# The high and low parts of the embedding rows: made per use by ScalarE and VectorE, or once by GpSimd and loaded

## The reference, cut to what matters

```
x1 = relu(x @ W_ah + b_ah)
for W, a_src, a_dst, b in the three layers:
    h = (x1 @ W).reshape(N, 4, 192)                  # the feature product
    e = leaky_relu((h*a_src).sum(-1)[src] + (h*a_dst).sum(-1)[dst], 0.2)
    p = exp(e - segment_max(e, dst)[dst]); alpha = p / segment_sum(p, dst)[dst]
    out = relu(segment_sum(alpha * h[src], dst) + b)
x = x + relu(concat(outs) @ W_out + b_out) + linear_attention(layernorm(x))
```

## Time and profile before

| | us |
|---|---|
| median of three runs | 1359.35 |
| the profiled execution itself | 1361.11 |
| its span in the trace | 1359.3 |
| TensorE busy | 1292.5 (95%) |
| VectorE busy | 984.1 (72%) |
| ScalarE busy | 509.4 (37%) |
| GpSimd busy | 44.1 (3%) |

### The profile page before, as it was taken

The page is one execution under the profiler, slowest core; times in us unless marked ns, Lnnn a source line. Parts: engine busy times, 40 slices in busy tenths (PEclk is TensorE's granted clock), DMA queues, the critical chain, the costliest instruction groups (busy, mean ns, idle before and its releaser), DMA issues.

```text
span 1359.3 us, 19970 instructions
## 1 busy us (share of the span) xinstructions
PE 1292.5 (95%) x7893; PEld 1220.7 (90%) x7893; DVE 984.1 (72%) x1703; ACT 509.4 (37%) x844; POOL 44.1 (3%) x52
## 2 busy tenths in 40 slices
PE   5899889999997999999999999999999999999886
PEld 5667559999996999999999999999999999999784
DVE  5667859999997526967766676677667766778577
ACT  4334232434345214443334333433343334333373
POOL 5000000000000500000000000000000000000000
PEclk9999989999998999999999999999999999999998
DMA  9210030222215847102011102110211011105003
GB/s 248 86 71 1 1 110 20 92 92 78 88 39 164 239 125 197 38 14 66 1 73 38 41 0 74 39 41 1 74 38 41 0 73 39 43 1 149 1 0 114
DMA packets 23510, 90.13 MB, mean 66 GB/s; under 512 B 3537, under 2 KB 4878, under 8 KB 20347
## 3 DMA queue, kind: packets, MB, share of 16 engines
q1 hardware_dynamic: 22495, 86.57, 19.9%
q10 hardware_dynamic: 924, 2.30, 0.6%
HBM read 77.80 MB, written 11.06 MB: 65 GB/s over the span
## 4 chain that ended last, share of the span: by engine, by line
PE 54%; DVE 7%; ACT 1%; issue 0%; DVEq 0%
PE psum L1763 26%; PE psum L105 9%; PE psum L106 8%; PE psum L107 8%; DVE hN L1383 2%; PE psum L1777 1%; DVE prob L1367 1%; DVE prob L1361 1%; PE psum L1817 1%; DVE acc L1500 0%; DVE acc L1405 0%; DVE x1l L1390 0%; PE psum L1832 0%; DVE acc L1421 0%; ACT prob L1591 0%
## 5 line engine op out<-in xcount | busy, mean ns | idle before, releaser
L1763 PE MATMUL psum<-hN,prob 125*125 125x193 f32 x2400 | 408.8, 327 | 0.0
L1763 PEld LDWEIGHTS psum<-hN,prob 125*125 125x125 f32 x2400 | 395.4, 187 | 0.2
L1591 ACT ACTIVATE prob<-prob,acol 125x1250 f32<-125x1250 f32 x120 | 160.9, 1341 | 378.8 <-DVE prob L1361 378.8
L1367 DVE SCALAR_TENSOR_TENSOR prob<-prob,cnt 125x1250 f32<-125x1250 f32 x120 | 174.6, 1455 | 56.3 <-ACT prob L1591 56.3
L1361 DVE SCALAR_TENSOR_TENSOR prob<-vrow,ncol,urow 125x1250 f32<-125x1250 f32 x120 | 181.7, 1515 | 9.5 <-PE psum L1763 9.5
L796 DVE CUSTOM_DVE_ANT_0 junk<-mask,arow 125x1250 bf16<-125x1250 uint8 x120 | 174.7, 1456 | 3.1
L105 PE MATMUL psum<-woh,xlh 128*125 128x384 f32 x360 | 128.0, 356 | 2.6 <-DVE acc L1405 2.6
L106 PE MATMUL psum<-wol,xlh 128*125 128x384 f32 x360 | 123.3, 343 | 0.0
L107 PE MATMUL psum<-woh,xll 128*125 128x384 f32 x360 | 122.6, 341 | 0.0
L105 PE MATMUL psum<-wph,x1h 128*125 128x384 f32 x330 | 117.6, 356 | 3.4 <-PEq L1018 1.9
L107 PE MATMUL psum<-wph,x1l 128*125 128x384 f32 x330 | 111.3, 337 | 0.0
(11 more groups left out here) (255 smaller groups left out, 2128.9 us busy)
## 6 DMA issues: line engine op xcount, KB each, us to landing
arow<-scratch_a SPq DMA_DIRECT2D x12, 625.0 KB, 3.9
urow<-scratch_uv SPq DMA_DIRECT2D x12, 625.0 KB, 4.4
vrow<-scratch_uv SPq DMA_DIRECT2D x12, 625.0 KB, 5.9
wT<-in_w_turned SPq DMA_DIRECT2D x6, 1152.0 KB, 7.4
wq_raw<-in_w_qkv SPq DMA_DIRECT2D x6, 1152.0 KB, 6.7
wp_raw<-in_w_pair SPq DMA_DIRECT2D x6, 1152.0 KB, 7.5
wo_raw<-in_w_out SPq DMA_DIRECT2D x6, 1152.0 KB, 5.3
xN<-in_x SPq DMA_DIRECT2D x10, 336.0 KB
```

The lines of the kernel that those rows point to most:

```text
L1367: nc.vector.scalar_tensor_tensor(prob[n % RING][:, :], prob[n % RING][:, :], 1.0, cnt[:, n % NT, :], op0=ALU.min, op1=ALU.mult).then_inc(p ...
L1591: nc.scalar.activation(prob[n % RING][:, :], prob[n % RING][:, :], ACT.Exp, bias=acol[:, n // NT, n % NT:n % NT + 1]).then_inc(e_ready, 1)
L1763: last = nc.tensor.matmul(bank(t // 2)[0:P, 193 * (t % 2):193 * (t % 2) + 193], ring[:, t * P:(t + 1) * P], hN[i % 2][:, j, 193 * s:193 * ...
```

## The change

The parts of the ten tiles of `x1` are made once. During attention GpSimd makes for each tile a high part (a cast) and a low part (a subtraction) in one buffer, `x1_in_store`, and SyncE stores it to device memory (`dram_x1`, 6000 bytes for each of 128 partitions, 750 KB a tile). GpSimd starts a tile when the store of the one before has landed. In the convolutions ScalarE starts a load of 750 KB for each feature product but the first, into two buffers in turn (`x1_both`), one of them where `x1T` was. `x1_high` and `x1_low` are gone from ScalarE and VectorE. A load waits until the product that last read its buffer is done.

```
--- before.py
+++ after.py
@@ -116,6 +116,7 @@
     dram_a, dram_low = scratch("a", (HEADS, N)), scratch("low", (HEADS, 1))
     dram_uv = scratch("uv", (2 * HEADS, N))
     dram_y = scratch("y", (PAIRS, 128, N))
+    dram_x1 = nc.dram_tensor("scratch_x1", (NT, 128, 2 * KT * P), F32, kind="Internal").ap()
     dram_res = scratch("res", (NT, P, D))
     ctx = ExitStack()
     with ctx:
@@ -162,8 +163,11 @@
         y_next = at("y_next", STAGE_AT + 41312, [128, N])
         wp_first = at("wp_raw", ACC_AT + 4 * NT * D + 99520, [128, KT * PC])
 
-        x1h = at("x1h", MASK_AT, [128, KT, P], F32R)
-        x1l = at("x1l", MASK_AT + 3008, [128, KT, P], F32R)
+        x1_in_store = at("x1_in_store", STAGE_AT + 68960, [128, 2 * KT * P])
+        x1_store = [x1_in_store[:, KT * P * q:KT * P * (q + 1)].bitcast(F32R).rearrange("p (k n) -> p k n", k=KT) for q in range(2)]
+        x1_both = [at(f"x1_both{b}", o, [128, 2 * KT * P]) for b, o in enumerate((MASK_AT, X1_AT))]
+        (x1h, x1l), (x1h_odd, x1l_odd) = [[both[:, KT * P * q:KT * P * (q + 1)].bitcast(F32R).rearrange("p (k n) -> p k n", k=KT)
+                                           for q in range(2)] for both in x1_both]
         wph = at("wph", ACC_AT + 4 * NT * D + 71104, [128, KT, PC], F32R)
         wpl = at("wpl", ACC_AT + 4 * NT * D + 99520, [128, KT, PC], F32R)
 
@@ -696,7 +700,7 @@
 
 
     at, xnh, xnl, mask, amax, bank = (g[k] for k in "at xnh xnl mask amax bank".split())
-    ident = g["ident"]
+    ident, x1T = g["ident"], g["x1T"]
     with ExitStack() as ctx:
         def sb(name, shape, dt=F32):
             return ctx.enter_context(nc.sbuf_tensor(name, shape, dt))
@@ -704,6 +708,7 @@
         def sem(name):
             return ctx.enter_context(nc.semaphore(name))
 
+        parts_ready, parts_out = sem("parts_ready"), sem("parts_out")
         w_raw, w_high, w_low = g["wq_raw"], g["wq_high"], g["wq_low"]
         S = STAGE_AT
         kf = at("kf", S, [P, NT, 128])
@@ -752,16 +757,23 @@
                 sp.wait_ge(y_ready, NG * (i + 1))
                 sp.dma_start(g["dram_y"][i], y[:, :]).then_inc(y_out, 16)
 
+            def store_parts(t):
+                sp.wait_ge(parts_ready, 2 * t + 2)
+                sp.dma_start(g["dram_x1"][t], g["x1_in_store"][:, :]).then_inc(parts_out, 16)
+
             a_row(0)
             a_row(1)
             for i in range(PAIRS):
                 if i + 1 < PAIRS:
                     weights(i + 1)
+                    store_parts(2 * i)
                     a_row(2 * i + 2)
                 if i:
                     store(i - 1)
                 if i + 1 < PAIRS:
                     a_row(2 * i + 3)
+                    store_parts(2 * i + 1)
+            sp.wait_ge(parts_out, 16 * NT)
             for k in range(2):
                 sp.dma_start(g["wp_first_raw"][k][:, :], g["w_proj"][:, PROJ[k], :]).then_inc(g["wproj_in"][k], 16)
             sp.wait_ge(y_out, 16)
@@ -780,6 +792,14 @@
                 nc.gpsimd.memset(blocks[b, 128 + h:129 + h], 1.0).then_inc(zeroed, 1)
                 pool.wait_ge(zeroed, 2 * h + 3)
             nc.gpsimd.memset(vf[:, :, 128:130], 1.0).then_inc(ones_col, 1)
+            high, low = g["x1_store"]
+            for t in range(NT):
+                here = x1T[:, :, t * P:(t + 1) * P]
+                if t:
+                    pool.wait_ge(parts_out, 16 * t)
+                nc.gpsimd.tensor_copy(high[:, :, :], here).then_inc(parts_ready, 1)
+                pool.wait_ge(parts_ready, 2 * t + 1)
+                nc.gpsimd.tensor_tensor(low[:, :, :], here, high[:, :, :].bitcast(F32), ALU.subtract).then_inc(parts_ready, 1)
 
         @block.vector
         def _(dve):
@@ -1206,8 +1226,8 @@
         S = ACC_AT + 4 * NT * D
 
         hN = [at(f"hN{i}", S + 15456 * i, [P, NT, PC + 2]) for i in range(2)]
-        x1h_odd = at("x1h_odd", S + 15456, [128, KT, P], F32R)
-        x1l_odd = at("x1l_odd", S + 15456 + 3008, [128, KT, P], F32R)
+        x1h_odd, x1l_odd, x1_both = (g[k] for k in "x1h_odd x1l_odd x1_both".split())
+        x1_in = [sem(f"x1_in{b}") for b in range(2)]
         gN = [h[:, :, 1:PC + 1] for h in hN]
         prob = [at(f"prob{i}", S + 30912 + 5024 * i, [P, N]) for i in range(RING)]
         urow = [at(f"urow{i}", S + 51008 + 10048 * i, [128, N]) for i in range(2)]
...
@@ -1270,8 +1290,8 @@
         def down_of(t):
             return max(d for d, (t0, n) in enumerate(DOWNS) if t0 <= t)
 
-        def x1_parts(i, t):
-            return (x1h_odd, x1l_odd) if i == 0 and t % 2 else (x1h, x1l)
+        def x1_parts(t):
+            return (x1h_odd, x1l_odd) if t % 2 else (x1h, x1l)
 
 
         @block.sync
@@ -1384,12 +1404,6 @@
                                                    total[:, t // 2, t % 2:t % 2 + 1], b_pair[0:P, C * s:C * (s + 1)],
                                                    op0=ALU.mult, op1=ALU.add).then_inc(g_ready, 1)
 
-            def x1_low(i, t):
-                dve.wait_ge(xh_ready, NT * i + t)
-                high, low = x1_parts(i, t)
-                nc.vector.tensor_tensor(low[:, :, :], x1T[:, :, t * P:(t + 1) * P], high[:, :, :].bitcast(F32), ALU.subtract)\
-                    .then_inc(xl_ready, 1)
-
             def out_low(i, t):
 
                 dve.wait_ge(t_high, NT * i + t + 1)
@@ -1513,8 +1527,6 @@
                         scores(tile + AHEAD)
                     if 0 <= i and tile + AHEAD - 1 < ALL:
                         weigh(tile + AHEAD - 1)
-                    if i + 1 < PAIRS and n >= NT and (i, n) not in ((-1, NT), (0, NT)):
-                        x1_low(i + 1, n - NT)
                     if i >= 1 and 2 <= n < NT + 2:
                         accumulate(i - 1, n - 2)
                     if 0 <= i and not lean and tile + AHEAD < ALL:
@@ -1526,8 +1538,6 @@
                     if i == -1 and EARLIER + AHEAD <= n < EARLIER + 2 * AHEAD - 1:
                         weigh(n - EARLIER - AHEAD)
                     if 0 <= i and n == NT - 1:
-                        if i == 0:
-                            x1_low(1, 0)
                         denominators(i, 0)
                         normalise(i, 0, range(NT))
                     if i >= 0 and n == TILES - 1:
@@ -1591,12 +1601,10 @@
                 nc.scalar.activation(prob[n % RING][:, :], prob[n % RING][:, :], ACT.Exp,
                                      bias=acol[:, n // NT, n % NT:n % NT + 1]).then_inc(e_ready, 1)
 
-            def x1_high(i, t):
-                if i:
-                    act.wait_ge(h_full, NT * i + t)
-                elif t >= 2:
-                    act.wait_ge(h_full, t - 1)
-                nc.scalar.activation(x1_parts(i, t)[0][:, :, :], x1T[:, :, t * P:(t + 1) * P], ACT.Copy).then_inc(xh_ready, 1)
+            def x1_load(i, t):
+                if NT * i + t >= 2:
+                    act.wait_ge(h_full, NT * i + t - 1)
+                act.dma_start(x1_both[t % 2][:, :], g["dram_x1"][t]).then_inc(x1_in[t % 2], 16)
 
             def take_h(i, t):
                 act.wait_ge(h_full, NT * i + t + 1)
@@ -1670,18 +1678,18 @@
                 for n in range(TILES):
                     tile = TILES * i + n
                     if i + 1 < PAIRS and n >= NT:
-                        if (i, n) not in ((-1, NT), (0, NT)):
-                            x1_high(i + 1, n - NT)
                         if n > NT:
                             take_h(i + 1, n - NT - 1)
+                        if n + 1 < TILES:
+                            x1_load(i + 1, n - NT + 1)
+                    if 0 <= i < PAIRS - 1 and n == NT - 1:
+                        x1_load(i + 1, 0)
                     if 0 <= i < PAIRS and n == 0:
                         take_h(i, NT - 1)
                     if 0 <= i and tile + AHEAD < ALL:
                         exponential(tile + AHEAD)
                     if i == -1 and EARLIER < n <= EARLIER + AHEAD:
                         exponential(n - EARLIER - 1)
-                    if (i, n) == (0, NT - 2):
-                        x1_high(1, 0)
                     if 1 <= i < PAIRS and n < NT:
                         out_high(i - 1, n)
                     if 0 <= i < PAIRS - 1 and n == 4:
@@ -1735,7 +1743,7 @@
                 if i and t == 0:
                     pe.wait_ge(wpl_ready, i)
                 if i or t:
-                    pe.wait_ge(xl_ready, NT * i + t)
+                    pe.wait_ge(x1_in[t % 2], 16 * (NT // 2 * i + t // 2 + t % 2))
                 if t >= 3:
                     pe.wait_ge(h_ready, NT * i + t - 2)
                 elif i >= 2:
@@ -1745,7 +1753,7 @@
                         pe.wait_ge(o_free, TILES * (i - 2) + TILES - 2 + t)
                 elif i == 1:
                     pe.wait_ge(h_ready, NT)
-                high, low = x1_parts(i, t)
+                high, low = x1_parts(t)
                 for k in range(KT):
                     last = split_matmul(nc, bank(5 + t % 3)[0:P, 0:PC], (high[:, k, :], low[:, k, :]),
```

60 lines of the change are left out of this document (34 added, 26 removed).

## The result

The changed kernel takes 1401.5 us (median; 1399.7 to 1404.3) against 1360.2 us for the kernel before on the same chip: a ratio of 1.030 (95% interval 1.0285 to 1.032), 41 us slower, where 1394 was forecast. The rest is read from one profiled execution of each; the changed kernel's has a span of 1398.6 us, 39.3 us more than before.

A forecast was written before the change was run, and what follows sets the result against it. TensorE was taken to bound the convolution periods and period -1, VectorE also attention; 21.3 + 14 - 1.6 + 0.9 = 34.6 us gave 1395.7 on the profiled execution, 1394 us as median; range for 8 in 10, 1371 to 1410.

The forecast's parts named there:

- the second term: Loads during the ten feature products before period 0: +14 us; wrong if products come less than 4 or more than 5.7 us apart.
- Attention: GpSimd's casts and subtractions take turns with VectorE's two-SBUF-input instructions: 21.3 us lost, bounds 0 and 26.
- L796 is free beside GpSimd: Rival in attention: this custom VectorE instruction doesn't take turns with GpSimd; attention costs some 3 us, time 1375; chance 0.15.
- less some 0.13 us for VectorE's own steps: In attention, deducted from GpSimd's whole 2.58 us per tile for VectorE's gaps between instructions, leaving 2.45 us lost per tile.
- Period -1: Ten feature products before period 0, loads waiting for one of two buffers: 4.8 us a tile, +14 us, bounds +7 and +22.
- The formula (product + take + load) / 2: Time per tile with two buffers before period 0: (3.2 + 0.5 + 5.9)/2 = 4.8 us.
- the 5.9 us put in for a load beside SyncE's queue: Before period 0, a 750 KB load beside other transfers: 3.6 us of moving plus 2.3 fixed, against 4.3 alone.
- half of 279 GB/s, 5.5 us: Upper bound before period 0: a load gets half the bandwidth, 768 kB in 5.5 us, 5.7 us a tile.
- The clock: Before period 0 TensorE, idle a third of the time, may get a lower clock; a risk inside the upper bound, unpriced.
- Gain in the periods: Periods 0 to 5: removing part-making from ScalarE and VectorE shortens TensorE's waits for `acc`, 1.6 us, at most 4.05.
- first product of pair 1: In period 0 its load, standing in ScalarE's list before the exponential, lands late: cost 0.9 us, bounds 0 and 2.
- Loads in the periods: From period 0 on, a load has 9 us against 4.3 needed, so hidden but once; late-loads rival 1440 us, chance 0.08.

The follow-up runs named there:

- the second experiment: Changed kernel, but GpSimd makes the parts of tile 0 only and the same buffer is stored ten times; all loads, stores and waits kept: 1387.9 us, ratio 1.019.

## Why the prediction was right, and where its terms were off

The time, the range and the sign held, but two of the terms were off in opposite directions, 6 us too much and 15 too little, and the gain was set 3 too low; another 2 us are differences in stages that the change doesn't touch. That these leave 39.3 us in the traces against a sum of 34.6 is in part luck. By its own signs of being wrong, the second term failed: the products of period -1 are 6.6 us apart, more than the 5.7 that it allowed.

- **Attention, 21.3 forecast, 15.3 measured.** The mechanism was right: the parts made on GpSimd alone give it, memsets don't. That L796 is free beside GpSimd is refuted. Tile 1 and eight later tiles lose 1.7 us each (two tiles a pair, 40.66 - 37.28 = 3.4 us), not 2.45. The step that failed is that the whole of GpSimd's work counts "less some 0.13 us for VectorE's own steps": VectorE has more than steps between its maxima, namely instructions without two SBUF inputs, and GpSimd runs beside those for nothing. ("L796 fills 30 of a pair's 37 us" should read 29, 20 times 1.456.) SyncE's waits cost at most the 1.2 us of the second experiment.
- **Period -1, 14 forecast, 29.5 measured**, outside the bounds of 7 and 22. The formula (product + take + load) / 2 was right within some 5%: with the 9.6 us of the trace, a median, it gives (3.2 + 0.5 + 9.6) / 2 = 6.65 us a tile, with the means of the nine products (3.8 us) and loads (8.4) it gives 6.35, and 59.2 / 9 = 6.6 was measured. The step that failed is the 5.9 us put in for a load beside SyncE's queue, and with it the upper bound "half of 279 GB/s, 5.5 us" (whose 5.7 us a tile come to +21 us, not 22). I took half of the bytes for the worst, but 768 kB in 9.6 us are 80 GB/s, well under half of the 289 that moved. In the sentence on packet turns, 6000 against 3072 bytes, the Trainium skill (DMA: Bandwidth & Descriptors, "Queues, rings and completion order") would have given an estimated 5.0 us a tile. The 6.6 us do not bear out single packets of that size taking plain turns; a packet on that page is a group of descriptors, so its rule isn't refuted. The trace has the packets of both queues (q1 is SyncE's, q10 ScalarE's with the loads; packets, MB, share), first in the changed kernel from 532.39 to 542.97 us, in which one load landed, then with four buffers from 522.24 to 532.01:

```profile
q1 hardware_dynamic: 616, 1.98, 74.0%
q10 hardware_dynamic: 175, 0.90, 28.8%
```

```profile
q10 hardware_dynamic: 407, 2.15, 53.7%
q1 hardware_dynamic: 409, 1.81, 47.2%
```

Where three loads are queued the two queues take turns one for one; a load by itself got one packet in four or five. Why it gets so few isn't shown. Without the broadcast the load is 4.4 us in the median and the loss 12.0. That this is near the forecast of 14 is chance: the forecast was made with the broadcast in place, and its formula gives 4.0 us a tile for such a load, where 4.6 was measured.
- **The clock** was named as a risk "inside the upper bound" and given no term. It is 7.4 of the 29.5 us. The earlier trace rows had a hint of its price, a granted clock of 0.87 in a stretch with 6.83 us of work in 15; here it is 0.80 with 37 in 59. A forecast of 14 us of idle TensorE should have carried a price for the products that follow a wait: 22.1 us of waits brought 7.4 here. With the broadcast later, 8.5 us of waits went with 3.5, but only 1.9 of them behind a wait for a load.
- **Gain in the periods, 1.6 forecast; first product of pair 1, 0.9 of loss.** Together the periods gained 3.4 us. The waits for `acc` fell from 2.6 to 1.0 us as said, but a period gained 0.58 us, 2.5 us in all with the order alone; most of the rest lies ahead of the first product of pair 1: from the tenth product to the eleventh it was 37.2 us and is 36.6. The load there was in time: ScalarE only issues it and goes on, so the exponential and the load started together (605.84), the load landed 4.3 us later, and the product began at 610.23 with no wait for it.
- **Loads in the periods** are hidden, as said: no wait for one after 580 us, and the loads of pairs 1 to 5 alone cost nothing (the experiment with period -1 as before).
- **What would show it**: GpSimd busy 76.7 us (70 said), row loads 40.7 us apart (42), L816 longer by 11.7 us in all (20), VectorE's busy time down by 31 us: 55.5 us of instructions are gone, 15 come back as waits inside L816 and L824, 4 lie in 19 small instructions of the first block (`shift`), where the change does nothing, and the rest is in small parts elsewhere.

The change as a whole then: 15 us for work on GpSimd that VectorE and ScalarE had room for in the convolutions, 29 us for loads with no lead, and 3.4 us back, of which 2.5 were to be had by exchanging two instructions.

## What to carry to other kernels

Before moving work to GpSimd, look at what VectorE reads at that time: here only its instructions with two SBUF inputs were held up, only by GpSimd instructions that read SBUF, and the gaps and the other instructions between were free. A load that replaces a computation must be issued earlier by its worst landing time beside all that shares the engines, not by its time alone; two more buffers, or moving one big transfer that nobody awaits, was worth 25 and 17 us, and both together 26. And where a stage is bound by TensorE, look first for the one instruction queued ahead of the sum it waits for: changing their order gave most of what removing the work gave.

## What the runs showed of the hardware that was not expected

- A small wait costs TensorE more than itself. A wait of 3.8 us was followed by a product of 5.5 us instead of 3.0, and in the changed kernel four of nine products ran so. It does not always: TensorE stands 1.9 us ahead of the first product of period -1 in all thirteen kernels. In four of them, two of which load nothing there, that product then took 4.4 to 4.6 us, in the other nine 3.1. A difference of 1.5 us between two traces in this place says nothing of the change.
- How much the transfer engines move at a full share depends on what is queued: 289 GB/s at 0.99 in the changed kernel's middle of period -1, 366 at 1.00 with three loads under way, 115 at 1.01 while the last 13 rows of the broadcast moved. First the changed kernel while rows, weights and loads move (packets of 5000 to 9216 bytes for the most part), then the kernel with the broadcast later while hardly anything else does (909 of 910 packets, of 3072 bytes):

```profile
524.00:532.00 8.00, 5.27 (x22) 4.96 (x21) 4.38 (x3) 0.49 (x1) 0.00 (x0) 0.79 1.03 427
566.00:578.00 12.00, 12.00 (x75) 12.00 (x74) 10.51 (x8) 6.22 (x5) 0.00 (x0) 1.00 1.02 234
```

At 234 GB/s the 3.84 MB of the broadcast take all engines an estimated 16 us, nearly twice what as many bytes of rows or parts take at 427: a broadcast weighs more on what runs beside it than its size says.
